# Another order of work inside a batch body: keys at steps 4 and 7, values together at step 5, sums of two steps joined

## The chip, the cores and the metric

One core of one Trainium2 chip. The time is device microseconds (us) of one execution; lower is better. The core has TensorE (PE, matrix products; its weight loads are shown as PEld), VectorE (DVE), ScalarE (ACT), GpSimd (POOL) and SyncE (SP, which here only issues DMAs). Each works through its own instruction list in order and waits on semaphores that the others raise.

## The reference

A block of three parts for 16 batches of 64 query tokens of width 128. Only the first part, a cross attention, is touched by the change:

```python
x = x + xattn(layernorm(x), ctx, ctx)        # ctx: (16 batches, 1601 keys, 128)
q, k, v = (t.reshape(b, -1, 16, 8).transpose(0, 2, 1, 3) for t in (x@Wq.T+bq, ctx@Wk.T+bk, ctx@Wv.T+bv))
weights = softmax(q @ k.T / sqrt(8))         # 16 heads of 8
out = (weights @ v) @ Wo.T + bo
x = x + mamba_mlp(layernorm(x), ...)         # state space model, then an MLP
x = x + experts(layernorm(x), ...)           # 8 gated experts, two chosen per token
```

## The kernel before, in words

`attention` runs 16 **bodies**, one for a batch (index `i`), each of 13 **steps** (`k`), one for every 128 keys (the last has 65). The order of everything is written out by hand and the same list of steps is walked by each engine. In one step TensorE does some of these:

- `scores(i, k)` (L647): 8 bf16 matmuls, transposed scores of 128 keys against 16 heads x 64 queries, into two of three halves `score`. ScalarE then does two exps (L836), one for each half (p = 0, 1), into `probs` (4 slots). `scores` of a step may start once the first exp of the step before is done.
- `sum_values(b, s)` (L667): weights times values of step s, with a column of ones for the denominators; fp32, into the bank `sums`. It needs both exps of s. At the end of a batch ScalarE copies `sums` out (`sums_out`, L826).
- `maxima(b, u)` (L596): unit u of 16 of a *later* batch: a rough pass of scores, 2 x 401 columns into one of the two buffers of `wide`, of which VectorE takes the row maximum (L911). After u = 15 come `row_maxima` (L920), `turn_max` (L604, a transpose) and `shifts` (L928, L930); SyncE sends the shift to `q_cur` (L352), and `scores` of the next batch needs it.
- `keys(i + 3, half)` (L515 to L517 with 401 columns): projection of the keys of a later batch, two halves, into `wide`; ScalarE copies each out (`keys_out`, L818) to `k_full`, GpSimd splits that into bf16 high and low parts (`split_keys`, L438, L441), SyncE lays them into `k_stack` (L320).
- `vals(i + 2, half)` (L515 to L517 with 128 columns): projection of the values, 7 and 6 blocks of 128 keys, into `wide`; VectorE copies each half out (`vals_out`, L907). GpSimd's `split(i + 4)` (L425, L428) waits for the second half.

`wide` is a **ring of two buffers**: the users come in the order of `ring_order()`, and each waits until the one two places before it has been emptied, by VectorE (units, values, turned maxima) or by ScalarE (keys).

A body in steady state before the change, as the loop at L695 and `units_at` with `LEAD = 5` give it (m = unit, s = sums of that step, s11 and s12 are of the batch before):

```
step  0: m7 s11      1: m8 s12     2: m9 values0     3: m10 s0 s1 m11    4: m12 s2
step  5: m13 s3 values1            6: m14 s4 keys0   7: m15 s5           8: m0 s6 keys1 m1
step  9: m2 s7 turn 10: m3 s8     11: m4 s9         12: m5 s10 m6
```

Bodies 1 to 12 have all of it. Body 0 has its own table (two units in each of steps 0 to 7, keys at 9 and 11, turn at 10, no values), body 13 has no keys, body 14 neither keys nor values, body 15 no units; bodies 14 and 15 also turn finished sums and project tokens (`tail_at`). ScalarE does `keys_out` and `sums_out` after both exps of their step.

Of the kernel before, what the change touches and what calls it, by code (L numbers as in the profile page):

```python
# [12 lines left out]
B, LQ, LK = 16, 64, 1601  # L13
# [11 lines left out]
NK = (LK + P - 1) // P  # L25
# [3 lines left out]
VW, VH = GH * HD + 2, GH - 1  # L29
NPROB, NSCORE, NSLOT, NQ = 4, 3, 3, 4  # L30
PREFETCH = 3
LEAD = 5
M_LOW, M_SIGN, M_FIRST = 2, 3, 4
V_STEPS, K_STEPS = (2, 5), (6, 8)
P_STEPS, C_STEPS = (3, 6), (8, 9, 11, 12)
TAIL = 10
NSPARE = 4
# [15 lines left out]
def keys_of(k):  # L53
    return min(P, LK - k * P)


def units_at(i, k):

    found = []
    for b in (i + 1, i + 2):  # L60
        lead = {1: 0, 2: 3}.get(b, LEAD)
        found += [(b, u) for u in range(16) if 1 <= b < B and
                  NK * (b - 1) - lead + (lead + 8) * u // 16 == NK * i + k]
    return found


def keys_at(i, k):

    steps = K_STEPS if i else (9, 11)
    return [(i + PREFETCH, steps.index(k))] if k in steps and i + PREFETCH < B else []  # L70


def turn_step(i):

    return 9 if i else 10


def tail_at(i, k):


    at = NK * (i - B + 2) + k - TAIL
    found = [("w", p, 0) for p in range(3) if at == 5 * p + 5]
    found += [("s", p, at - 5 * p) for p in range(3) if at in (5 * p, 5 * p + 1)]
    return found + [("o", p, 0) for p in range(3) if at == 5 * p + 4]
# [15 lines left out]
def ring_order():  # L100

    order = [("k", 0, 0), ("k", 0, 1), ("x", 0, 0), ("q", 0, 0)]
    order += [("m", 0, u) for u in range(16)] + [("t", 0, 0), ("v", 2, 0), ("v", 2, 1)]
    for i in range(B):
        for k in range(NK):
            order += [("m",) + unit for unit in units_at(i, k)[:1]]
            if k in V_STEPS and 0 < i < B - 2:
                order += [("v", i + 2, V_STEPS.index(k))]
            order += [("k",) + half for half in keys_at(i, k)]
            order += [("m",) + unit for unit in units_at(i, k)[1:]]  # L110
            if k == turn_step(i) and i + 1 < B:
                order += [("t", i + 1, 0)]
            order += [what for what in tail_at(i, k) if what[0] != "w" and what[2] == 0]
    return order
# [27 lines left out]
def attention(nc, A, keep):  # L142


    with ExitStack() as ctx:
# [366 lines left out]
        def _(pe):  # L512
# [52 lines left out]
            def keys(b, half):  # L565
                n, w = b % 2, half_free(pe, ("k", b, half))
                if b == 0:
                    pe.wait_ge(s_low0, half + 1)
                elif half == 0:
                    pe.wait_ge(s_split, b)  # L570
                for c in range(2):
                    at = CH * (2 * half + c)
                    last = product3(wide[:, w, 512 * c:512 * c + CH], wkv_hi[:, 0, :], wkv_lo[:, 0, :],
                                    ctx_hi[:, n, at:at + CH], ctx_lo[:, n, at:at + CH])
                last.then_inc(s_wide, 1)

            def vals(b, half):
                n, w = b % 2, half_free(pe, ("v", b, half))
                for k in range(7 * half, 7 + 6 * half):
                    at = P * (k - 7 * half)  # L580
                    ks = slice(k * P, k * P + P)
                    last = product3(wide[:, w, at:at + P], ctx_hi[:, n, ks], ctx_lo[:, n, ks],
                                    wkv_hi[:, 1, :], wkv_lo[:, 1, :])
                last.then_inc(s_wide, 1)
# [69 lines left out]
            def sum_values(b, k):  # L654
                n, m, slot = b % NSLOT, keys_of(k), (NK * b + k) % NPROB
                if k == 0:
                    if b < 2:
                        spare_emptied(pe, ("v", b, 3))
                    else:
                        is_empty(pe, ("v", b, 1))  # L660
                    if b:
                        pe.wait_ge(s_sums, b)
                pe.wait_ge(s_exp, 2 * (NK * b + k) + 2)
                for c, (first, heads) in enumerate(((0, VH), (VH, 1))):
                    for g in range(G):
                        q = (GH * g + first) * LQ
                        last = pe.matmul(sums[32 * g:32 * g + 32, first * LQ:(first + heads) * LQ],  # L667
                                         values[0:m, n, k, VW * g + 2 * c:VW * g + 2 * c + 32],
                                         probs[0:m, slot, q:q + heads * LQ],
                                         start=(k == 0 and c == 0), stop=(k == NK - 1), skip_group_check=True)  # L670
                last.then_inc(s_pv, 1)
# [23 lines left out]
            for i in range(B):  # L695
                for k in range(NK):
                    scores(i, k)
                    units = units_at(i, k)
                    if units:
                        maxima(*units[0])  # L700
                    if i >= 1 and k < 2:
                        sum_values(i - 1, NK - 2 + k)
                    if k == 3:
                        sum_values(i, 0)
                    if k >= 3:
                        sum_values(i, k - 2)
                    if k in V_STEPS and 0 < i < B - 2:
                        vals(i + 2, V_STEPS.index(k))
                    for half in keys_at(i, k):
                        keys(*half)  # L710
                    for unit in units[1:]:
                        maxima(*unit)
                    if k == turn_step(i) and i + 1 < B:
                        turn_max(i + 1)
                    for kind, p, t in tail_at(i, k):
                        if kind == "s":
                            turn_sums(p, t)
                        elif kind == "o":
                            turn_tokens(p)
                        else:  # L720
                            project_tokens(p)
# [6 lines left out]
        def _(act):  # L728
# [93 lines left out]
            def sums_out(b):  # L822
                act.wait_ge(s_pv, NK * (b + 1))
                if b == 0:
                    act.wait_ge(s_qlow, len(LATE_Q))
                nc.scalar.copy(keep.sums[:, :, b * LQ:b * LQ + LQ],  # L826
                               sums[:, 0:GH * LQ].rearrange("p (j q) -> p j q", j=GH)).then_inc(s_sums, 1)

            for i in range(B):
                for k in range(NK):  # L830
                    m, step = keys_of(k), NK * i + k
                    for p in range(2):
                        act.wait_ge(s_score, 2 * step + p + 1)
                        if p == 0 and step >= NPROB:
                            act.wait_ge(s_pv, step - NPROB + 1)
                        nc.scalar.activation(  # L836
                            probs[0:m, step % NPROB, :].rearrange("r (g p c) -> r p g c", g=G, p=2)[:, p],
                            score[0:m, (2 * step + p) % NSCORE, :].rearrange("r (g c) -> r g c", g=G), ACT.Exp,
                            scale=HD ** -0.5).then_inc(s_exp, 1)
                    if i >= 1 and k == 1:  # L840
                        sums_out(i - 1)
                    for half in keys_at(i, k):
                        keys_out(*half)
            sums_out(B - 1)
            nc.scalar.activation(root_of_one[:], one[:], ACT.Sqrt)

# [1 line left out]
        def _(dve):  # L848
# [164 lines left out]
            for i in range(B):  # L1013
                for k in range(NK):
                    units = units_at(i, k)
                    for b, u in units[:1]:
                        maximum(b, u)
                        if u == 15:
                            row_maxima(b)
                    if k in V_STEPS and 0 < i < B - 2:  # L1020
                        vals_out(i + 2, V_STEPS.index(k))
                    for b, u in units[1:]:
                        maximum(b, u)
                        if u == 15:
                            row_maxima(b)
                    if k == turn_step(i) and i + 1 < B:
                        shifts(i + 1)
                    for kind, p, t in tail_at(i, k):
                        if kind == "s":
                            if t == 1:  # L1030
                                divide(p)
                        elif kind == "o":
                            tokens_out(p)
                        else:
                            residual(p)
# [1142 lines left out]
```

## Time and profile before

| | |
|---|---|
| median of 3 runs (lowest to highest) | 572.72 us (571.77 to 573.69) |
| the profiled execution: its time | 574.46 us |
| its span, first to last instruction | 572.6 us |
| busy: PE, PEld, DVE, ACT, POOL | 91%, 59%, 73%, 66%, 57% |

The span is shorter than the execution's time by what lies around the instructions. Attention takes the first 386 us or so; the two later parts are not touched. Busy shares are averages over all stages; a busy PE is not a PE at its peak, since matmuls overlap. In the timeline a row is: start, length, engine, line, operation, how many were merged, and in brackets how long the engine was idle before it and whose work ended that.

### The profile page before, as it was taken

To read this page: it belongs to the slowest core of one execution; us is meant where nothing else is said; L and a number is where in the kernel's file an instruction comes from. 1 tells how busy PE (TensorE), PEld (TensorE's weight loads), DVE (VectorE), ACT (ScalarE), POOL (GpSimd) and SP (SyncE) were. 2 spreads that over 40 slices of the span, in tenths; PEclk is the share of its full clock that TensorE was granted. 3 is DMA by queue.
4 is the path that set the end of the run, shared out by engine and by line. 5 is a ranking of instruction groups with operands and counts; after the bars stand their busy time and mean duration, and the time that the engine had idled before them with its cause. 6 is when DMAs were issued, how large, how long until landed. Compare 5 with 4: busy or idle time off the path is not lost. (4 is left out here: it accounts for less than half of the span.)

```text
span 572.6 us, 18926 instructions
## 1 busy us (share of the span) xinstructions
PE 520.9 (91%) x7882; PEld 338.6 (59%) x7882; DVE 419.7 (73%) x749; ACT 380.4 (66%) x704; POOL 323.6 (57%) x197
## 2 busy tenths in 40 slices
PE   3887999999999999999999999999999869999997
PEld 1534565565565565565565565665375736777776
DVE  6287888797797798788788799447877567455554
ACT  4883668678678678778778778873844426656662
POOL 1698878558558558558657299204000035667673
PEclk9897999999999999999999999999989979999999
DMA  6776444354354354354352463002000000000001
GB/s 210 137 154 132 124 112 96 91 119 93 87 121 96 81 120 97 83 119 98 81 119 49 107 145 84 3 2 101 2 1 2 1 1 1 2 2 0 0 0 38
DMA packets 17962, 41.64 MB, mean 73 GB/s; under 512 B 5542, under 2 KB 8366, under 8 KB 17770
## 3 DMA queue, kind: packets, MB, share of 16 engines
q1 hardware_dynamic: 17144, 40.10, 30.2%
q8 instruction: 59, 0.97, 0.8%
q10 hardware_dynamic: 740, 0.42, 0.2%
q14 instruction: 19, 0.16, 0.1%
HBM read 19.70 MB, written 0.52 MB: 35 GB/s over the span
## 5 line engine op out<-in xcount | busy, mean ns | idle before, releaser
L911 DVE TENSOR_REDUCE half_max<-wide 128x2 f32<-128x802 f32 x256 | 241.6, 988 | 42.8 <-PE wide L596 38.8
L836 ACT ACTIVATE probs<-score 128x512 f32<-128x512 f32 (+1 forms) x416 | 225.8, 596 | 66.6 <-PE score L647 66.3
L667 PE MATMUL sums<-probs,values 128*32 128x192 f32 (+3 forms) x3328 | 131.6, 280 | 0.0
L667 PEld LDWEIGHTS sums<-probs,values 128*32 128x32 f32 (+1 forms) x3328 | 86.9, 110 | 51.4 <-issue 22.6
L596 PE MATMUL wide<-k_stack,q_cur 48*128 48x401 bf16 x512 | 87.5, 339 | 12.6 <-ACT k_full L818 6.2
L647 PE MATMUL score<-q_cur,k_stack 50*128 50x128 bf16 (+1 forms) x1664 | 82.7, 219 | 7.3 <-ACT probs L836 6.3
L425 POOL TENSOR_TENSOR ctx_hi<-ctx_in,one 128x1601 bf16<-128x1601 f32 x15 | 42.9, 2857 | 76.9 <-PE wide L517 67.8
L1904 POOL TENSOR_TENSOR hid_lo<-hid_e,hid_hi 114x512 bf16<-114x512 f32 x47 | 54.1, 1156 | 35.5 <-ACT hid_hi L1928 34.3
L647 PEld LDWEIGHTS score<-q_cur,k_stack 50*128 50x128 bf16 (+1 forms) x1664 | 51.9, 95 | 32.7 <-ACT probs L836 12.9
L2039 DVE SCALAR_TENSOR_TENSOR hid_e<-gu,keep_bgu,gate 114x512 f32<-114x512 f32 x48 | 35.9, 750 | 40.1 <-ACT gate L1941 40.0
L438 POOL TENSOR_TENSOR k_hi<-k_full,one 128x1601 bf16<-128x1601 f32 x15 | 42.8, 2856 | 31.0 <-ACT k_full L818 24.9
L1941 ACT ACTIVATE gate<-gu,gate_bias 114x512 f32<-114x512 f32 x48 | 32.9, 687 | 37.0 <-PE gu L1874 34.7
L428 POOL TENSOR_TENSOR ctx_lo<-ctx_in,ctx_hi 128x1601 bf16<-128x1601 f32 x15 | 48.6, 3242 | 1.2
L441 POOL TENSOR_TENSOR k_lo<-k_full,k_hi 128x1601 bf16<-128x1601 f32 x15 | 48.6, 3239 | 1.2
L596 PEld LDWEIGHTS wide<-k_stack,q_cur 48*128 48x128 bf16 x512 | 24.8, 93 | 38.1 <-DVE half_max L911 16.7
L1872 PE MATMUL gu<-keep_t_hi,keep_w_hi 128*114 128x512 bf16 x96 | 37.6, 392 | 4.9 <-DVE hid_e L2039 4.9
L907 DVE COPY values<-wide 128x896 f32<-128x896 f32 (+1 forms) x28 | 28.7, 1024 | 15.4 <-PE wide L517 15.3
L818 ACT ACTIVATE k_full<-wide,keep_vecs 128x802 f32<-128x802 f32 x26 | 24.2, 929 | 22.1 <-PE wide L517 22.1
L1873 PE MATMUL gu<-keep_t_lo,keep_w_hi 128*114 128x512 bf16 x96 | 37.3, 389 | 0.0
L1874 PE MATMUL gu<-keep_t_hi,keep_w_lo 128*114 128x512 bf16 x96 | 37.2, 388 | 0.0
L515 PE MATMUL wide<-wkv_hi,ctx_hi 128*128 128x128 bf16 x182 | 33.4, 225 | 2.9 <-DVE half_max L911 2.9
L1889 POOL MEMSET one<- 114x1 f32 x1 | 0.1, 99 | 63.5 <-POOLq L1043 63.5
(327 smaller groups left out, 919.1 us busy)
## 6 DMA issues: line engine op xcount, KB each, us to landing
k_stack<-k_hi SPq DMA_DIRECT2D x128, 102.0 KB, 3.4
ctx_in<-in_ctx SPq DMA_DIRECT2D x56, 200.1 KB, 3.4
k_stack<-k_lo SPq DMA_DIRECT2D x64, 102.0 KB, 3.2
ctx_in<-in_wgu SPq DMA_DIRECT2D x16, 171.0 KB, 3.4
keep_w<-in_w SPq DMA_DIRECT2D x1, 1368.0 KB
ctx_in<-in_ctx SPq DMA_DIRECT2D x1, 800.5 KB, 8.4
keep_x<-in_x SPq DMA_DIRECT2D x1, 512.0 KB, 7.0
q_cur<-shift SPq DMA_DIRECT2D x30, 2.0 KB
```

What stands on the lines that cost most here:

```text
L425: pool.tensor_tensor(ctx_hi[:, n, 0:LK], ctx_in[:, n, :], one[:].to_broadcast([P, LK]), ALU.mult).then_inc(s_splithi, 1)
L428: pool.tensor_tensor(ctx_lo[:, n, 0:LK], ctx_in[:, n, :], ctx_hi[:, n, 0:LK], ALU.subtract).then_inc(s_split, 1)
L438: pool.tensor_tensor(k_hi[:, 0:LK], k_full[:, 0:LK], one[:].to_broadcast([P, LK]), ALU.mult).then_inc(s_khi, 1)
L441: pool.tensor_tensor(k_lo[:, 0:LK], k_full[:, 0:LK], k_hi[:, 0:LK], ALU.subtract).then_inc(s_klo, 1)
L596: last = pe.matmul(wide[:, w, 512 * p:512 * p + CH], q_cur[half:half + TERM, b % NQ, g].rearrange("p h q -> p (h q)"), k_stack[half:half + ...
L647: last = pe.matmul(score[0:m, (2 * step + p) % NSCORE, P * g:P * g + P], k_stack[half:half + TERM + 2, n, g, k * P:k * P + m], q_cur[half: ...
L667: last = pe.matmul(sums[32 * g:32 * g + 32, first * LQ:(first + heads) * LQ], values[0:m, n, k, VW * g + 2 * c:VW * g + 2 * c + 32], probs ...
L836: nc.scalar.activation(probs[0:m, step % NPROB, :].rearrange("r (g p c) -> r p g c", g=G, p=2)[:, p], score[0:m, (2 * step + p) % NSCORE, ...
L911: dve.tensor_reduce(half_max[:, b % 2, :, u // 4, u % 4], wide[:, w, :].rearrange("p (c k) -> p c k", c=2)[:, :, 0:CH], AX.X, ALU.max).the ...
L1872: pe.matmul(o, hi, t_hi[:, half], start=True, stop=False)
L1873: pe.matmul(o, hi, t_lo[:, half], start=False, stop=False)
L1904: pool.tensor_tensor(hid_lo[:, par, h, n, :], hid[:, n, :], hid_hi[:, par, h, n, :], ALU.subtract).then_inc(s["lo"], 1)
```

## The change

The steps get a new table; no operation is added or taken away. In steady state:

```
step  0: m6 s11 m7   1: s12 m8     2: m9 s0 s1 m10   3: s2 m11           4: keys0 m12 s3
step  5: m13 values0 values1       6: m14 s4 s5      7: m15 keys1        8: m0 s6 turn
step  9: m1 s7 m2   10: s8 m3     11: m4 s9         12: m5 s10
```

The units of batches 1 and 2 keep their places. On ScalarE `keys0` is now copied out between the two exps of its step, `keys1` after them, and `sums_out` between the two exps of step 1.

```diff
-LEAD = 5
-V_STEPS, K_STEPS = (2, 5), (6, 8)
+V_STEP, K_STEPS = 5, (4, 7)
+UNIT_STEPS = (8, 9, 9, 10, 11, 12, 13, 13, 14, 15, 15, 16, 17, 18, 19, 20)
+SUM_STEPS = (2, 2, 3, 4, 6, 6, 8, 9, 10, 11, 12, 13, 14)
+SUMS_BEFORE_MAXIMA = (1, 3, 10)
...
-        lead = {1: 0, 2: 3}.get(b, LEAD)
-        found += [(b, u) for u in range(16) if 1 <= b < B and
-                  NK * (b - 1) - lead + (lead + 8) * u // 16 == NK * i + k]
+        lead = {1: 0, 2: 3}.get(b)
+        found += [(b, u) for u in range(16) if 1 <= b < B and NK * i + k == (
+            NK * (b - 2) + UNIT_STEPS[u] if lead is None else NK * (b - 1) - lead + (lead + 8) * u // 16)]
+def sums_at(i, k):
+    return [(b, s) for b in (i - 1, i) if b >= 0 for s in range(NK) if NK * (b - i) + SUM_STEPS[s] == k]
 def turn_step(i):
-    return 9 if i else 10
+    return 8 if i else 10
...
                     scores(i, k)
                     units = units_at(i, k)
+                    for b, half in keys_at(i, k):
+                        if half == 0:
+                            keys(b, half)
+                    if k in SUMS_BEFORE_MAXIMA:
+                        for b, s in sums_at(i, k):
+                            sum_values(b, s)
                     if units:
                         maxima(*units[0])
-                    if i >= 1 and k < 2:
-                        sum_values(i - 1, NK - 2 + k)
-                    if k == 3:
-                        sum_values(i, 0)
-                    if k >= 3:
-                        sum_values(i, k - 2)
-                    if k in V_STEPS and 0 < i < B - 2:
-                        vals(i + 2, V_STEPS.index(k))
-                    for half in keys_at(i, k):
-                        keys(*half)
+                    if k == V_STEP and 0 < i < B - 2:
+                        for half in range(2):
+                            vals(i + 2, half)
+                    for b, half in keys_at(i, k):
+                        if half == 1:
+                            keys(b, half)
+                    if k not in SUMS_BEFORE_MAXIMA:
+                        for b, s in sums_at(i, k):
+                            sum_values(b, s)
                     for unit in units[1:]:
                         maxima(*unit)
...
                             scale=HD ** -0.5).then_inc(s_exp, 1)
-                    if i >= 1 and k == 1:
-                        sums_out(i - 1)
-                    for half in keys_at(i, k):
-                        keys_out(*half)
+                        if i >= 1 and k == 1 and p == 0:
+                            sums_out(i - 1)
+                        for b, half in keys_at(i, k):
+                            if half == p:
+                                keys_out(b, half)
```

`ring_order()` and VectorE's loop follow the same table.

## Rows read from the trace of the kernel before

**Rows 1.** Timeline of DVE, the `shifts` of bodies 1, 12 and 13
```profile
92.76 0.27 DVE L928 CAST shift_hi<-wide 16x128 bf16<-16x128 f32 x1
...
327.56 0.27 DVE L928 CAST shift_hi<-wide 16x128 bf16<-16x128 f32 x1
346.27 0.27 DVE L928 CAST shift_hi<-wide 16x128 bf16<-16x128 f32 x1
```
**Rows 2.** Busy time by stretch: one whole body
```profile
221.14:242.48 21.34, 20.10 (x399) 12.87 (x397) 17.82 (x23) 15.90 (x30) 13.98 (x7) 1.00 0.45 100
```
**Rows 3.** Timeline of PE in that stage: two plain steps
```profile
200.48 0.40 PE L647 MATMUL score<-q_cur,k_stack 50*128 50x128 bf16 x8
200.72 0.34 PE L596 MATMUL wide<-k_stack,q_cur 48*128 48x401 bf16 x2
200.98 0.65 PE L667 MATMUL sums<-probs,values 128*32 128x192 f32 x16
201.56 0.41 PE L647 MATMUL score<-q_cur,k_stack 50*65 50x128 bf16 x8
```
**Rows 4.** Timeline of PE: values (step 2), joined sums and an extra unit (step 3)
```profile
205.94 0.10 PEld L515 LDWEIGHTS wide<-wkv_hi,ctx_hi 128*128 128x128 bf16 x1 [0.48 <-DVE half_max L911]
...
207.22 0.40 PE L647 MATMUL score<-q_cur,k_stack 50*128 50x128 bf16 x8
...
207.72 1.08 PE L667 MATMUL sums<-probs,values 128*32 128x192 f32 x32
208.73 0.34 PE L596 MATMUL wide<-k_stack,q_cur 48*128 48x401 bf16 x2
208.91 0.39 PE L647 MATMUL score<-q_cur,k_stack 50*128 50x128 bf16 x8
```
**Rows 5.** Timeline of PE: keys (step 6), then the turn (step 9)
```profile
213.53 0.34 PE L515 MATMUL wide<-ctx_hi,wkv_hi 128*128 128x401 bf16 x1
...
214.66 0.40 PE L647 MATMUL score<-q_cur,k_stack 50*128 50x128 bf16 x8
...
220.27 0.38 PE L604 MATMUL wide<-nident,row_max 128*16 128x128 f32 x2
220.59 0.40 PE L647 MATMUL score<-q_cur,k_stack 50*128 50x128 bf16 x8
```
**Rows 6.** Timeline of PE in body 0, scores followed at once by sums
```profile
64.01 0.39 PE L647 MATMUL score<-q_cur,k_stack 50*128 50x128 bf16 x8
64.33 0.64 PE L667 MATMUL sums<-probs,values 128*32 128x192 f32 x16
```
**Rows 7.** Waits, 199.24 to 220.58 us (one body): us in total, times, longest
```profile
PEld score L647 <- ACT probs L836: 0.8, 2, 0.6
PEld wide L596 <- ACT k_full L818: 0.7, 1, 0.7
PEld wide L596 <- DVE half_max L911: 0.6, 3, 0.2
```
**Rows 8.** Timeline of ACT: `sums_out`, `keys_out`
```profile
205.49 0.38 ACT L826 COPY keep_sums<-sums 128x256 f32<-128x256 f32 x1
...
218.55 0.93 ACT L818 ACTIVATE k_full<-wide,keep_vecs 128x802 f32<-128x802 f32 x1 [0.80 <-PE wide L517]
219.38 1.08 ACT L836 ACTIVATE probs<-score 128x512 f32<-128x512 f32 x2
```
**Rows 9.** Timeline of DVE: units back to back, a copy of values
```profile
200.28 6.50 DVE L911 TENSOR_REDUCE half_max<-wide 128x2 f32<-128x802 f32 x7
207.32 1.09 DVE L907 COPY values<-wide 128x896 f32<-128x896 f32 x1 [0.54 <-PE wide L517]
```
**Rows 10.** Timeline of POOL: first of `split`, last of `split_keys`
```profile
212.63 2.86 POOL L425 TENSOR_TENSOR ctx_hi<-ctx_in,one 128x1601 bf16<-128x1601 f32 x1 [6.45 <-PE wide L517]
...
222.49 3.25 POOL L441 TENSOR_TENSOR k_lo<-k_full,k_hi 128x1601 bf16<-128x1601 f32 x1
```
**Rows 11.** Busy time by stretch, in body 0 (columns as in rows 2)
```profile
54.90:58.00 3.10, 3.10 (x48) 1.86 (x46) 2.20 (x3) 0.83 (x3) 3.02 (x2) 0.53 0.88 143
```

More of the change, by code:

```diff
@@ L105, in ring_order @@
         for k in range(NK):
+            order += [("k",) + half for half in keys_at(i, k) if half[1] == 0]
             order += [("m",) + unit for unit in units_at(i, k)[:1]]
-            if k in V_STEPS and 0 < i < B - 2:
-                order += [("v", i + 2, V_STEPS.index(k))]
-            order += [("k",) + half for half in keys_at(i, k)]
+            if k == V_STEP and 0 < i < B - 2:
+                order += [("v", i + 2, half) for half in range(2)]
+            order += [("k",) + half for half in keys_at(i, k) if half[1] == 1]
             order += [("m",) + unit for unit in units_at(i, k)[1:]]
@@ L698, in _ @@
                     units = units_at(i, k)
+                    for b, half in keys_at(i, k):
[4 more added lines that the diff above has]
+                            sum_values(b, s)
                     if units:
                         maxima(*units[0])
-                    if i >= 1 and k < 2:
-                        sum_values(i - 1, NK - 2 + k)
-                    if k == 3:
-                        sum_values(i, 0)
-                    if k >= 3:
-                        sum_values(i, k - 2)
-                    if k in V_STEPS and 0 < i < B - 2:
-                        vals(i + 2, V_STEPS.index(k))
-                    for half in keys_at(i, k):
-                        keys(*half)
+                    if k == V_STEP and 0 < i < B - 2:
+                        for half in range(2):
[6 more added lines that the diff above has]
+                            sum_values(b, s)
                     for unit in units[1:]:
@@ L1019, in _ @@
                             row_maxima(b)
-                    if k in V_STEPS and 0 < i < B - 2:
-                        vals_out(i + 2, V_STEPS.index(k))
+                    if k == V_STEP and 0 < i < B - 2:
+                        for half in range(2):
+                            vals_out(i + 2, half)
                     for b, u in units[1:]:
```

## The prediction
> **What bounds the kernel now.** I read the page for the place of the change, then the timeline of VectorE for the period of a body, the busy time of one body, TensorE's timeline through one body, and last the waits of that body.
>
> The shifts of bodies 1 and 12 lie 327.56 - 92.76 = 234.80 us apart, eleven bodies: 21.345 us for a body; the next, without keys, takes 18.71 [rows 1]. In one body the engines are busy 20.10 (PE), 12.87 (PEld), 17.82 (DVE), 15.90 (ACT), 13.98 (POOL), and the granted clock is 1.00, which is 2.4 GHz [rows 2]. Nothing is full by busy time, so I count what TensorE must issue, from start to start of its instructions:
>
> - scores to unit 0.24, unit to sums 0.26, sums to next scores 0.58: a plain step is 1.08 [rows 3]. The two exps of a step take 1.08 on ACT as well [rows 8], so ACT has no slack in a plain step and much in a long one.
> - Values, 7 blocks: 205.94 to 207.22, 1.28; by blocks the second half is 6/7 of it, 1.10. Joined sums 1.01 instead of 2 x 0.58 = 1.16, saving 0.15. An extra unit at the end of a step 0.18 [rows 4].
> - Half the keys 1.13, the turn 0.32 [rows 5]. Scores followed at once by sums 0.32 [rows 6], so a step with the sums first is 0.32 + 0.58 + 0.18 = 1.08 too.
>
> A body before has 13 plain steps' worth (14.04), 3 extra units (0.54), two halves of keys (2.26), values (2.38), the turn (0.32), less one joined sum (0.15): 19.39. The period is 21.345, so TensorE stands still for **1.95 us a body**. The waits say where: for exps 0.8 (scores after a key copy), for `k_full` 0.7 (the unit behind keys1 in step 9), for VectorE 0.6 in three units [rows 7], and 0.48 ahead of values0 [rows 4]. That makes 2.6, more than 1.95 because a late weight load is partly covered by matmuls still running. TensorE is the bound at 91%, and every wait is for a buffer that an evacuating engine still holds.
>
> A rule speaks against this reading. The Trainium skill, Perfetto Trace Analysis, section Identifying the Most-Contended Engine, says that TensorE's matmul busy share is no good measure and that the load share is to be used; by it TensorE (12.87 of 21.34, 60%) would be far from full and VectorE (83%) the engine to relieve. It would leave up to 3.5 us a body to gain, not 1.95. The trace agrees that busy time overstates PE, but small moving tiles keep it from issuing faster than the starts above.
>
> **The change, part by part.** No instruction is added. What TensorE must issue in a body: 19.39 less another 0.15 for the second joined pair = 19.24. By step, 0 to 12: 1.26, 1.08, 1.69, 1.08, 2.21, 2.88, 1.51, 1.63, 1.40, 1.26, 1.08, 1.08, 1.08. For the waits I walk once through the ring and the exps. Rates: a reader starts 0.10 after TensorE's next start (207.22 to 207.32) and units on DVE are 0.92 apart, 0.99 long; the sixth of the seven ends at 205.87 and values start at 205.94, so a buffer comes back 0.07 after its reader ends [rows 4, 9]. Values copies 1.09 and about 1.0 [rows 9]. A key copy is 0.93, an exp can start 0.83 after it [rows 8]. Zero is the scores of step 5.
>
> - **Step 5**, m13 0.24, values0 0.50, values1 1.78, end 2.88. m13's reduce ends at 1.60, before values1. The copies end at 2.97 and 3.95. ACT has its two exps only and then idles some 1.5 us: no cost, as its 15.90 busy leave 4 us a body. Before, each half of values cost a wait or an ACT gap of its own.
> - **Step 6**, m14 at 3.12 finds the copied buffer back at 3.04; its reduce waits behind the second copy, 3.95 to 4.94. Joined sums keep TensorE busy meanwhile; step 7 starts at 4.39.
> - **Step 7**, m15 4.63, keys1 wants m14's buffer at 4.89 and gets it at 5.01: **wait 0.12**. Step 8 starts 6.14.
> - **Step 8**, keys1 is copied 6.25 to 7.18. The turn needs that buffer (7.25) and TensorE comes to it at 7.22. The exp queued behind the copy runs 7.08 to 7.62, and scores 9 need it: 7.69 against 7.54, **wait 0.15**. What was 0.5 ahead of step 8's scores and 0.5 behind keys1 is now covered by sums 6 and the turn.
> - **Steps 9 to 12**, DVE: m0, the two shifts (together about 0.75), m1 from 8.55, m2 ends 10.46. m4 wants its buffer at 10.27 and gets 10.53: **wait 0.26**. Step 0 starts 12.45.
> - **Steps 0 to 4**, `sums_out` (0.38 [rows 8]) sits between the exps of step 1, from about 1.05 after its scores, and ends before sums 0 start at 1.6; with the old place on ACT it would end near 2.0 and be late. m7's reduce ends at 15.06, m9 wants that buffer at 15.03: **wait 0.10**. Exps of step 2 end about 0.2 before sums 2 want them. keys0 in step 4 goes ahead of m12, whose buffer waits for nothing. Its copy delays only the second exp, and sums 4 come two steps later. Step 5 starts at 19.87.
>
> Waits 0.63 a body, period 19.87. Four places pass with under 0.1 to spare (m13 behind the key copy, m14, keys0, the turn); bounds for them are 0 and 0.1 each, and I take 0.10 in all. Period 19.97, **gain 1.38 us a body, 16.6 us in the 12 full bodies**.
>
> The rest: body 13 keeps the values and loses no key; step 7 then has neither sums nor keys and is held at 1.08 by the exps instead of 0.50, so it gains less, 0.6 (bounds 0 and 1.2). Bodies 14 and 15 are held by the exps; two joined pairs instead of one are longer on TensorE than on ACT by up to 0.4, and the steps without sums give nothing back: +0.5 together (0 to 1). Body 0 is held by VectorE with two units a step, 0. There the clock stands at 0.53 for 3.1 us (1.2 GHz for nearly all of it), after a stretch in which TensorE had only scores and units [rows 11]; sums one step earlier could shift or shorten it: -1.5 to +1, taken as 0. Sum: -16.6 - 0.6 + 0.5 = **-16.7 us**.
>
> Other queues: SyncE's steps are tied to the scores, so they contract with the body. The turn one step earlier puts the shift's DMAs some 3.5 us ahead of the scores that need it. GpSimd's `split` still starts when values end; in the timeline `k_lo` ends 225.74 - 212.63 = 13.1 us after it starts [rows 10], and with the keys earlier it no longer waits for them.
>
> Span 572.6 - 16.7 = 555.9, time of that execution 574.46 - 16.7 = 557.8; against the median, which is 1.7 lower, **556.0 us**.
>
> **Rivals.**
>
> - *VectorE becomes the bound.* My walk leaves it about 2 us idle a body, and two of four waits are already for it, with the 11 units from step 9 to step 3 at 0.92 filling 10.1 us in which TensorE issues 10.0. If each handover is slower, or the shifts or the second copy of values push the queue back by another 0.2 or so in three or four places, a body takes 20.6: gain 0.7 x 12 and the rest as above, 564. For: its 17.82 busy. Against: it idles before units and copies now. The skill's rule above would favour it, and by that rule the trace is not yet decided. Chance 0.2.
> - *All near misses pass.* Waits 0.4 a body and the slow clock in body 0 gone: 12 x 1.7 + 1.5 = 22, so 551. Chance 0.1.
> - *Slower, through k_full.* `keys_out` of half 0 may overwrite `k_full` only when GpSimd has written `k_lo` of the batch before, and it now sits between two exps: if it waits, the second exp, then the scores of step 6, wait with it. `split` starts at about 3.1, so `k_lo` ends near 3.1 + 13.1 - 0.7 = 15.5; the copy comes at 17.66 + 0.24 + 1.24 = 19.1. The room falls to 3.6 us; before, it was 213.53 + 21.34 + 1.24 - 225.74 = 10.4. Above 3.6 every further us of lateness is a us a body; from 5.0 the kernel is slower; at 6, 12 x 1 = 12 us more, 585. For: the keys moved two steps earlier, the values ended later. Against: GpSimd's operations have kept one duration all along. With whatever else turns the sign: chance 0.07.
> - *Nothing moves*: TensorE is full by its starts and the waits only change place, period near 21.3, 573. It would need 1.3 us of waits that the walk doesn't show. Chance 0.03.
>
> **How the numbers follow.** Forecast 0.6, VectorE bound 0.2, near misses pass 0.1, slower 0.07, nothing 0.03. The likeliest case by itself is 552 to 560; the range goes to the middle of the VectorE case and the edge of the better one, 551 to 564. Faster by over 0.3% (1.7 us, about what can be told from no change): 0.9; within it 0.03; slower 0.07.
>
> **What would show it.** Shifts 20.0 us apart (20.6: VectorE). PE busy per body unchanged near 20. The wait of a unit for `k_full` (0.7) and of the values for `half_max` (0.5) gone; small waits of units for `half_max` in steps 11 and 2; an ACT gap of some 1.5 us in each step 6. GpSimd's wait ahead of `k_hi` (before: for `k_full`) gone. A wait of `k_full` for GpSimd's `k_lo` would prove the slower case; a period above 20.3 would make the walk wrong, and its step is the one whose wait stands longest in the list.

## The result and the profile after

| | before | changed |
|---|---|---|
| median (lowest to highest) | 573.21 us (571.77 to 574.86), 4 runs | 556.0 us (552.94 to 559.36), 4 runs |
| ratio to before | | 0.9706, 95% interval 0.9677 to 0.9736 |
| the profiled execution: time, span | 574.46, 572.6 | 557.50, 555.7 |
| busy: PE, PEld, DVE, ACT, POOL | 91%, 59%, 73%, 66%, 57% | 92%, 61%, 76%, 69%, 58% |

The kernel is 3% faster, and its median is the predicted 556.0 us. Ratios here and below are of fast runs alone (of all runs one, 576.95 us in the first experiment, was slow). Each experiment had the kernel before run beside it (medians 571.53, 572.56 and 573.26 us for the three groups), so experiments are compared by ratio and by period, and their times only roughly.

The period of a body in the timeline of VectorE, as in [rows 1]:

```profile
92.86 0.27 DVE L946 CAST shift_hi<-wide 16x128 bf16<-16x128 f32 x1
...
310.13 0.27 DVE L946 CAST shift_hi<-wide 16x128 bf16<-16x128 f32 x1
328.72 0.27 DVE L946 CAST shift_hi<-wide 16x128 bf16<-16x128 f32 x1
```

Eleven bodies take 310.13 - 92.86 = 217.27 us, 19.75 each, against 21.345: **1.60 us less a body**. Busy time of one body (columns as in [rows 2]: the stretch, its length, then the busy time of PE, PEld, DVE, ACT and POOL with the count of instructions, and last the granted clock, the share of time the DMA engines work and GB/s):

```profile
191.61:211.36 19.75, 19.62 (x397) 12.98 (x397) 17.90 (x23) 16.01 (x31) 13.93 (x7) 1.00 0.44 108
```

VectorE, ScalarE and GpSimd are busy for what they were before, within 0.11 us, in a body 1.6 us shorter, at the same clock. PE shows 19.62 instead of 20.10; the prediction had it unchanged. The waits of that body, to be set beside [rows 7]:

```profile
PEld sums L679 <- ACT probs L853: 0.8, 4, 0.2
...
PEld score L659 <- ACT probs L853: 0.7, 2, 0.4
PEld wide L527 <- DVE half_max L929: 0.5, 2, 0.3
...
PEld wide L608 <- DVE half_max L929: 0.3, 1, 0.3
```

The unit's wait for `k_full` is gone, the 0.48 ahead of values is 0.25, the longest wait of scores for an exp fell from 0.6 to 0.4 (in total only from 0.8 to 0.7). Step 5 and what follows, PE:

```profile
203.80 0.40 PE L659 MATMUL score<-q_cur,k_stack 50*128 50x128 bf16 x8
204.04 0.35 PE L608 MATMUL wide<-k_stack,q_cur 48*128 48x401 bf16 x2
204.39 0.23 PE L527 MATMUL wide<-wkv_hi,ctx_hi 128*128 128x128 bf16 x1
...
206.67 0.40 PE L659 MATMUL score<-q_cur,k_stack 50*128 50x128 bf16 x8
206.92 0.34 PE L608 MATMUL wide<-k_stack,q_cur 48*128 48x401 bf16 x2
207.19 1.08 PE L679 MATMUL sums<-probs,values 128*32 128x192 f32 x32
208.21 0.40 PE L659 MATMUL score<-q_cur,k_stack 50*128 50x128 bf16 x8
...
209.84 0.40 PE L659 MATMUL score<-q_cur,k_stack 50*128 50x128 bf16 x8
210.07 0.34 PE L608 MATMUL wide<-k_stack,q_cur 48*128 48x401 bf16 x2
210.34 0.65 PE L679 MATMUL sums<-probs,values 128*32 128x192 f32 x16
210.93 0.39 PE L616 MATMUL wide<-nident,row_max 128*16 128x128 f32 x2
211.42 0.40 PE L659 MATMUL score<-q_cur,k_stack 50*128 50x128 bf16 x8
```

Both halves of the values run through in 2.28 us without a gap; the keys of step 7 too. One stop is ahead of the last row, 0.49 after the turn instead of 0.32: the scores wait for the exp behind the key copy. Another is ahead of the turn itself, which starts 0.59 after its sums, where before the change it started 0.46 after them (219.81 to 220.27): the copy of keys1 ends at 209.95 + 0.93 = 210.88, and the turn, which needs that buffer, starts at 210.93. The same on ACT and DVE:

```profile
207.10 1.09 ACT L853 ACTIVATE probs<-score 128x512 f32<-128x512 f32 x2 [1.66 <-PE score L659]
208.64 1.08 ACT L853 ACTIVATE probs<-score 128x512 f32<-128x512 f32 x2 [0.45 <-PE score L659]
209.95 0.93 ACT L835 ACTIVATE k_full<-wide,keep_vecs 128x802 f32<-128x802 f32 x1 [0.22 <-PE wide L529]
210.77 2.16 ACT L853 ACTIVATE probs<-score 128x512 f32<-128x512 f32 x4
```

```profile
205.77 1.96 DVE L925 COPY values<-wide 128x896 f32<-128x896 f32 x2 [0.35 <-PE wide L529]
207.65 0.98 DVE L929 TENSOR_REDUCE half_max<-wide 128x2 f32<-128x802 f32 x1
...
212.16 10.29 DVE L929 TENSOR_REDUCE half_max<-wide 128x2 f32<-128x802 f32 x11
```

The ACT gap behind the values is 1.66 us, and VectorE works eleven units on end, those issued from step 9 to step 3.

**Where 16.9 us of span went.** I cut both profiles at the scores of step 12 (65 rows high, `50x65`), the last of each body. Examples, of before and then of the changed kernel:

```profile
71.67 0.41 PE L647 MATMUL score<-q_cur,k_stack 50*65 50x128 bf16 x8
...
94.83 0.41 PE L647 MATMUL score<-q_cur,k_stack 50*65 50x128 bf16 x8
```

```profile
73.93 0.41 PE L659 MATMUL score<-q_cur,k_stack 50*65 50x128 bf16 x8
...
96.45 0.41 PE L659 MATMUL score<-q_cur,k_stack 50*65 50x128 bf16 x8
```

| stretch | before | changed | difference |
|---|---|---|---|
| to the first scores | 49.35 | 49.79 | +0.44 |
| body 0 | 22.32 | 24.14 | +1.82 |
| body 1 | 23.16 | 22.52 | -0.64 |
| bodies 2 to 12 | 234.80 | 217.27 | -17.53 |
| body 13 | 18.71 | 18.58 | -0.13 |
| bodies 14, 15 | 33.53 | 34.37 | +0.84 |
| all behind the attention | 190.7 | 189.0 | -1.7 |

The code of the first row and the last is untouched, so these differences are not the change's. The low clock of body 0 lay elsewhere in the two profiles (before at 54.9 to 58, [rows 11]) and lasted longer in the second; after:

```profile
50.00:54.00 4.00, 3.47 (x34) 1.32 (x29) 3.30 (x4) 2.54 (x5) 4.00 (x3) 0.50 0.42 95
54.00:58.00 4.00, 4.00 (x72) 2.54 (x70) 2.59 (x4) 1.80 (x4) 3.92 (x3) 0.66 0.65 144
```

### The profile page after: what moved, and what is told of

It is laid out like the page before. It is cut to its first block and busy times, and to the rows that moved or that the text cites. A ratio compares the mean times of both kernels' runs of the same rounds, so it can differ in the third digit from the quotient of the medians.

```text
span 555.7 us, 18926 instructions
## 1 busy us (share of the span) xinstructions
PE 512.7 (92%) x7882; PEld 338.8 (61%) x7882; DVE 419.9 (76%) x749; ACT 382.0 (69%) x704; POOL 323.0 (58%) x197
## 5 line engine op out<-in xcount | busy, mean ns | idle before, releaser
L679 PE MATMUL sums<-probs,values 128*32 128x192 f32 (+3 forms) x3328 | 128.0, 279 | 0.0
L527 PE MATMUL wide<-wkv_hi,ctx_hi 128*128 128x128 bf16 x182 | 31.4, 220 | 0.5 <-DVE half_max L929 0.5
L1851 PE MATMUL down<-w_hi,hid_hi 114*128 (+1 forms) x180 | 31.7, 219 | 0.0
```

## The experiments

The numbers measured are the period of a steady body, from shift to shift, and the time. The first six each undo one part of the change and leave the rest; the first also contains the edit of the sixth, the order of sums and unit inside a step.

**Sums by the old table.**

```diff
-SUM_STEPS = (2, 2, 3, 4, 6, 6, 8, 9, 10, 11, 12, 13, 14)
-SUMS_BEFORE_MAXIMA = (1, 3, 10)
+SUM_STEPS = (3, 3, 4, 5, 6, 7, 8, 9, 10, 11, 12, 13, 14)
+SUMS_BEFORE_MAXIMA = ()
```

> The changed kernel, but the sums as before: sums 0 and 1 joined at step 3, the sums of step k-2 at step k, always behind the first unit. In the changed kernel a steady body takes 19.75 us (shift to shift). My theory, that TensorE's own issue time plus its waits make the body: one joined pair less costs 0.15, and sums now stand behind 2.4 us of values (step 5) or keys (step 7), so the exps late after a key copy are no longer covered: 20.1 to 20.6, whole time 4 to 10 us above 556. Rival, the joining brings only the 0.15 us of TensorE that it saves: 19.90, 2 us above.

Measured: 21.25 a body (195.21 to 216.47), 573.66 us, ratio to before 1.003 (1.0003 to 1.0057). Nearly the whole gain is gone, 1.50 of 1.60 us a body, more than either theory said; the time is above both as well. (The profiled execution, 567.40 us, was the fastest of ten.) Its PE timeline shows what I had left out: step 2 now holds scores and two units, 0.65 us of work, and takes 1.55, held by VectorE and the exps; the sums it might have done make steps 3, 5 and 7 longer.

```profile
202.68 0.40 PE L659 MATMUL score<-q_cur,k_stack 50*128 50x128 bf16 x8
202.91 0.34 PE L608 MATMUL wide<-k_stack,q_cur 48*128 48x401 bf16 x2
203.63 0.34 PE L608 MATMUL wide<-k_stack,q_cur 48*128 48x401 bf16 x2 [0.38 <-DVE half_max L929]
204.23 0.40 PE L659 MATMUL score<-q_cur,k_stack 50*128 50x128 bf16 x8 [0.26 <-ACT probs L853]
```

Step lengths against the changed kernel: step 2 -0.15, 3 +0.52, 5 +0.57, 6 -0.45, 7 +0.65, 8 -0.30, 9 to 1 +0.6 together. Sums moved out of a step that is then short give nothing back; in the step they move to they cost 0.52 to 0.65. About 0.5 of the 1.5 is the order of sums and unit, which the sixth experiment takes alone.

**Keys at steps 6 and 8.**

```diff
-V_STEP, K_STEPS = 5, (4, 7)
+V_STEP, K_STEPS = 5, (6, 8)
```

> The changed kernel, but keys at steps 6 and 8 again. My theory: the turn (step 8) must now wait for the copy of the keys issued in the same step, and the joined sums of step 6 delay the keys; waits on key copies come back, body 20.4 to 20.9, 564 to 570 us. Rival, the place of the keys is indifferent because ScalarE has 3.7 us of slack in a body: 19.8, 556 to 557.

Measured: 20.75, 570.52 us (just above my range), 0.9984 (0.9957 to 1.0012). The period is in my range and half of the cause is as I had it: waits behind key copies come back. But the turn does not wait (it starts 0.47 after its sums), and values wait for VectorE, which I had not foreseen, because the keys no longer stand ahead of them in step 4. The longest waits of TensorE in that body are 0.80 of scores for an exp and 0.74 of values for a unit's buffer:

```profile
207.56 0.10 PEld L527 LDWEIGHTS wide<-wkv_hi,ctx_hi 128*128 128x128 bf16 x1 [0.74 <-DVE half_max L929]
...
213.67 0.23 PEld L659 LDWEIGHTS score<-q_cur,k_stack 50*128 50x128 bf16 x8 [0.80 <-ACT probs L853]
```

**Values at steps 2 and 5.**

```diff
-            if k == V_STEP and 0 < i < B - 2:
-                order += [("v", i + 2, half) for half in range(2)]
+            if k in V_STEPS and 0 < i < B - 2:
+                order += [("v", i + 2, V_STEPS.index(k))]
```

(and the same in TensorE's and VectorE's loops, with `V_STEPS = (2, 5)`)

> The changed kernel, but the halves of the values at steps 2 and 5 again. My theory: step 2 lies inside VectorE's unbroken run of units, so the values must wait there for a buffer (0.4 to 0.6 as before the change) and steps 5 to 7 lose nothing: body 20.1 to 20.5, 560 to 565 us. Rival, that VectorE is the bound and its order of copies and maxima is indifferent: 19.75 +- 0.1, 556.

Measured: 20.60 and 568.42 us, both above my ranges, 0.9943 (0.9921 to 0.9965). The wait of the values is where I put it, in VectorE's run of units, but 0.94 instead of 0.4 to 0.6:

```profile
203.50 0.10 PEld L527 LDWEIGHTS wide<-wkv_hi,ctx_hi 128*128 128x128 bf16 x1 [0.94 <-DVE half_max L928]
```

**Units and turn at their old steps.**

```diff
-UNIT_STEPS = (8, 9, 9, 10, 11, 12, 13, 13, 14, 15, 15, 16, 17, 18, 19, 20)
+UNIT_STEPS = (8, 8, 9, 10, 11, 12, 12, 13, 14, 15, 16, 16, 17, 18, 19, 20)
...
-    return 8 if i else 10
+    return 9 if i else 10
```

> The changed kernel, but the units of batches from 3 on at their old steps (u1 with u0 at step 8, u6 at 12, u10 and u11 at 3) and the turn at step 9. My theory: each moved unit brings a wait of 0.1 to 0.2 for VectorE where two units meet a short step: body 19.95 to 20.3, 558 to 562 us. Rival, the units' table does not matter as VectorE has to do 16 of them in any case: 19.75.

Measured: 20.86, 571.69 us, 1.0004 (0.9982 to 1.0025): 1.11 of 1.60 us a body gone, where I expected 0.2 to 0.55, and by the time the whole gain; bodies 13 and 14 are each 1.0 to 1.1 us longer too. Units 10 and 11 both stand in step 3, right ahead of keys0 of step 4, which needs unit 10's buffer: TensorE stands still for most of a reduce, and step 4 is 3.07 us long instead of 2.31, which is 0.76 of the 1.11.

```profile
207.46 0.10 PEld L527 LDWEIGHTS wide<-ctx_hi,wkv_hi 128*128 128x128 bf16 x1 [0.87 <-DVE half_max L929]
```

**ScalarE's copies after both exps.**

```diff
-                        if i >= 1 and k == 1 and p == 0:
-                            sums_out(i - 1)
-                        for b, half in keys_at(i, k):
-                            if half == p:
-                                keys_out(b, half)
+                    if i >= 1 and k == 1:
+                        sums_out(i - 1)
+                    for b, half in keys_at(i, k):
+                        keys_out(b, half)
```

> The changed kernel, but ScalarE copies keys and sums out after both exps of their step, as before. My theory: the copy of the sums then ends about 2.0 after the scores of step 1 and the joined sums 0 of step 2 want their bank at 1.6, a wait of 0.3 to 0.4; the copy of keys0 starts 0.3 later and m13 waits as long: body 20.2 to 20.5, 561 to 565 us. Rival, ScalarE's order inside a step is hidden by the other half of the scores: 19.75 to 19.85, 556 to 557.

Measured: 20.05, 561.75 us, 0.9812 (0.9768 to 0.9856). The period is between both theories. The joined sums do wait for the copy of `sums`: they start 0.56 after the unit ahead of them instead of 0.27, and step 2 is 1.99 us long instead of 1.69, the whole 0.30. But m13 doesn't wait: both exps of step 4 end at 205.89, and keys0 is copied from 205.93, 0.10 behind m12's start as in the changed kernel, so the copy starts no later.

**The unit always first.**

```diff
-SUMS_BEFORE_MAXIMA = (1, 3, 10)
+SUMS_BEFORE_MAXIMA = ()
```

> The changed kernel, but the sums never ahead of the first unit (steps 1, 3 and 10 as the others). Steady body: sums 12 come 0.26 later, so the copy of the sums too, and units 8 and 11 ask for their buffer 0.6 earlier, when VectorE still has it: 19.9 to 20.2. In body 0 step 10 the unit is no longer held up behind the sums and the turn behind it comes sooner: 0.3 to 0.7 us less there. Whole: 557 to 560 us. Rival, the order of sums and units inside a step is indifferent: 19.75 in the body, and body 0 as it is.

Measured: 20.235, 559.78 us, 0.977 (0.9721 to 0.9819). The body as in my theory, a little above its range: steps 1, 2 and 10 are 0.18, 0.12 and 0.30 longer, step 11 is 0.13 shorter. In body 0 step 10 goes from 2.67 us to 1.98 (65.93 to 67.91 us), the 0.7 expected.

**Batches 0, 14 and 15 with the old table of sums.**

```diff
+EDGE_STEPS = (3, 3, 4, 5, 6, 7, 8, 9, 10, 11, 12, 13, 14)
...
-    return [(b, s) for b in (i - 1, i) if b >= 0 for s in range(NK) if NK * (b - i) + SUM_STEPS[s] == k]
+    return [(b, s) for b in (i - 1, i) if b >= 0 for s in range(NK)
+            if NK * (b - i) + (SUM_STEPS if 0 < b < B - 2 else EDGE_STEPS)[s] == k]
...
+def sums_first(i, k):
+    return k in SUMS_BEFORE_MAXIMA and (0 < i < B - 2 or i == B - 2 and k == 1)
...
-                    if k in SUMS_BEFORE_MAXIMA:
+                    if sums_first(i, k):
...
-                    if k not in SUMS_BEFORE_MAXIMA:
+                    if not sums_first(i, k):
```

> The changed kernel, but batches 0, 14 and 15 have the old table of sums (joined at step 3 only) and the sums go behind the unit in their bodies. The changed kernel's body 0 is 1.4 us, bodies 14 and 15 together 0.9 us longer than before the change in the two profiles. My theory: this is the table (joined sums that TensorE can't hide, steps 5 and 7 held by the exps), so bodies 14 and 15 lose 0.9 and body 0 at least 0.6: 1.5 to 2.3 us off, about 554. Rival, body 0's loss is where the slow clock fell, which changes from run to run: then only 0.9 off.

Measured: 19.75, 554.96 us, 0.9711 (0.9678 to 0.9743). Body 0, from its first scores to those of step 12, is 22.75 instead of 24.14; step 10 is 1.99 us in place of 2.67. Bodies 14 and 15 hardly gain: 16.66 and 17.46 against 16.46 and 17.91, 0.25 together where I expected 0.9. My theory is right for step 10 of body 0 and wrong for the last two bodies. The other 0.71 of body 0 lies in steps 0 to 7, where the clock is low for a while, and is not shown to be the table's: the profiles of the changed kernel and of the second to fourth experiments, whose code for body 0 is the same, take 23.95 to 24.85 us for it. By its time the kernel can't be told from the changed one, the intervals being nearly the same.

**Less work for TensorE.**

```diff
-                    last = product3(wide[:, w, 512 * c:512 * c + CH], wkv_hi[:, 0, :], wkv_lo[:, 0, :],
-                                    ctx_hi[:, n, at:at + CH], ctx_lo[:, n, at:at + CH])
+                    o = wide[:, w, 512 * c:512 * c + CH]
+                    pe.matmul(o, wkv_hi[:, 0, :], ctx_hi[:, n, at:at + CH], start=True, stop=False)
+                    last = pe.matmul(o, wkv_hi[:, 0, :], ctx_lo[:, n, at:at + CH], start=False, stop=True)
```

> The changed kernel with the third product of the keys (high part of the context times low part of the weights) left out in the 12 to 13 bodies that project keys in the ring: four matmuls of 401 columns, 0.17 us apart, 0.69 us of TensorE a body; its keys are less precise. If TensorE is the bound: 19.1 to 19.3 a body, 548 to 550 us. If VectorE is the bound: 19.65 to 19.75, 555 us or more.

Measured: 19.35 (188.62 to 207.97), 550.95 us, 0.9643 (0.9602 to 0.9684). 0.40 of 0.69 us comes through, a little less than the theory of a TensorE bound had. By steps: step 7 is 0.34 shorter, step 4 only 0.20, and step 11 grows by 0.13, its unit waiting for VectorE. So TensorE is the bound in most of the places where this work lies, not in all.

**Less work for VectorE.**

```diff
-                                  wide[:, w, :].rearrange("p (c k) -> p c k", c=2)[:, :, 0:CH],
+                                  wide[:, w, :].rearrange("p (c k) -> p c k", c=2)[:, :, 0:CH - 40],
```

> The changed kernel with each of VectorE's maxima taken over 2 x 361 instead of 2 x 401 columns (the last 40 of each half are left out, so the shift may be smaller than the true maximum): 16 reduces of 0.99 become about 0.91, some 1.3 us of VectorE less a body. If TensorE bounds the body and VectorE counts only in the 0.5 us of waits that TensorE has for it: 19.3 to 19.6 a body, 550 to 554 us. If VectorE is the bound (its 17.9 us and its turn-arounds): 18.4 to 18.8. Taking 0.69 us off TensorE gave 0.40.

Measured: 19.56, 550.13 us, 0.9626 (0.9575 to 0.9676). VectorE's busy time falls by 1.03 us (expected: 1.3) and the body by 0.19:

```profile
187.35:206.91 19.56, 19.44 (x397) 12.90 (x397) 16.87 (x23) 16.01 (x31) 13.93 (x7) 1.00 0.45 110
```

A microsecond off TensorE is worth 0.58 (0.40 / 0.69), one off VectorE 0.18 (0.19 / 1.03). No run takes work off ScalarE. In the plain steps its two exps take 1.08 us, as long as TensorE's starts, and in the body shown it works from 210.77 to 218.42 us, through steps 9 to 12, 0 and 1, with two gaps of 0.16 and 0.18 us. So these steps may be bound by ScalarE as much as by TensorE; which one is not shown. The time is lower than eleven bodies at 0.19 make it. In its profile the scores of step 12 of body 0 come 3.0 us earlier than in the changed kernel's (70.96 against 73.93): 1.9 of this lies ahead of the first scores, which come at 47.93 instead of 49.79, and 1.1 in body 0, where VectorE has two units a step and the low clock falls differently, which I can't tell apart. Bodies 1, 13 and 14 are 1.1 us shorter together.

**The new table of sums alone, in the kernel before.**

```diff
+SUM_STEPS = (2, 2, 3, 4, 6, 6, 8, 9, 10, 11, 12, 13, 14)
...
-                    if i >= 1 and k < 2:
-                        sum_values(i - 1, NK - 2 + k)
-                    if k == 3:
-                        sum_values(i, 0)
-                    if k >= 3:
-                        sum_values(i, k - 2)
+                    for b in (i - 1, i):
+                        for s in range(NK):
+                            if b >= 0 and NK * (b - i) + SUM_STEPS[s] == k:
+                                sum_values(b, s)
```

> The kernel before the change with the new table of sums alone (joined at steps 2 and 6; none at 5 and 7). All other work stands where it was. Undoing one part of the change each time took back 0.3 to 1.5 us of a body, 5.2 in all, while the whole brings 1.6; so the parts should be worth little alone. Here step 7 has only a unit and is held by the exps at 1.08 instead of 0.5, and sums 0 and 1 stand behind the values of step 2: 21.3 to 22.0 a body (before 21.345), 571 to 580 us. Rival, parts that each pay: 1.5 less at once, 19.9.

Measured: 22.65 (208.79 to 231.44), 590.82 us, 1.0294 (1.0244 to 1.0343): one part of the change alone makes the kernel 3% slower, more than my range said. Against the kernel before, the steps that gained sums grow: step 2, with values and the joined sums, by 1.05 (to 3.09 us), and step 6 by 0.40; step 4, with as much as before, by 0.26. The steps that have less now give back 0.25 (step 3), 0.13 (step 5) and 0.01 (step 7). Step 7:

```profile
225.28 0.40 PE L648 MATMUL score<-q_cur,k_stack 50*128 50x128 bf16 x8
225.51 0.34 PE L597 MATMUL wide<-k_stack,q_cur 48*128 48x401 bf16 x2
226.85 0.40 PE L648 MATMUL score<-q_cur,k_stack 50*128 50x128 bf16 x8 [1.01 <-ACT probs L835]
```

TensorE has only scores and a unit there, while ScalarE copies the keys of step 6 and only then does the exp that the next scores need; taking 0.58 us of sums out of the step turned them into waiting.

**Units of batch 2 on the new table too.** On top of the seventh:

```diff
+UNIT_STEPS_2 = (10, 10, 11, 11, 12, 12, 13, 13, 14, 15, 15, 16, 17, 18, 19, 20)
...
-        lead = {1: 0, 2: 3}.get(b)
-        found += [(b, u) for u in range(16) if 1 <= b < B and NK * i + k == (
-            NK * (b - 2) + UNIT_STEPS[u] if lead is None else NK * (b - 1) - lead + (lead + 8) * u // 16)]
+        found += [(b, u) for u in range(16) if 1 <= b < B and NK * i + k == (
+            u // 2 if b == 1 else NK * (b - 2) + (UNIT_STEPS if b > 2 else UNIT_STEPS_2)[u])]
```

> The kernel of e7 (batches 0, 14 and 15 with the old table of sums), and the units of batch 2 brought onto the new table from step 0 of body 1 on: u0 to u5 in pairs at steps 10, 11 and 12 of body 0, one more than before in body 0. Body 1 takes 22.5 us in the changed kernel against 19.75 of the next ones. If that is the shifted units of batch 2: body 1 20.0 to 20.8, body 0 longer by about 0.9 (one unit more for VectorE), 552.5 to 554 us. Rival, body 1 is long for what body 0 leaves late (stacks, keys): it stays at 22 or more, 555 to 556.

Measured: 553.78 us, 0.9656 (0.962 to 0.9693). Body 1 20.86 instead of 22.52, at the edge of my range; body 0 22.94 against 22.75 in the seventh, so the extra unit cost 0.2 rather than 0.9.

**And the first of them one step earlier.**

```diff
-UNIT_STEPS_2 = (10, 10, 11, 11, 12, 12, 13, 13, 14, 15, 15, 16, 17, 18, 19, 20)
+UNIT_STEPS_2 = (9, 10, 10, 11, 12, 12, 13, 13, 14, 15, 15, 16, 17, 18, 19, 20)
```

> As e11, but the first unit of batch 2 at step 9 of body 0 already, u1 and u2 at 10, u3 at 11, u4 and u5 at 12. VectorE stands idle in steps 8 and 9 of body 0, so the extra unit costs nothing there: 0.5 to 1 us better than e11. Rival, the unit shares the ring with keys0 of step 9 and delays them and the exps behind: equal to e11 or up to 1 us worse.

Measured: 552.87 us, 0.9665 (0.9623 to 0.9708). Bodies 0 and 1 together take 91.61 - 48.19 = 43.42 us against 46.66 in the changed kernel:

```profile
71.22 0.41 PE L666 MATMUL score<-q_cur,k_stack 50*65 50x128 bf16 x8
91.61 0.41 PE L666 MATMUL score<-q_cur,k_stack 50*65 50x128 bf16 x8
```

Against the eleventh it is 0.4 us the better over these two bodies, less than profiles of the same code for body 0 differ by, so neither theory is told from the other. It has the lowest median of the versions with full work, 3 us under the changed kernel, but by ratio the eleventh is as good (0.9656), and both intervals overlap the changed kernel's (0.9677 to 0.9736), so that they beat it is likely and not shown.

## Why the prediction was right, step by step

**The bound.** That TensorE's starts fill most of the body holds: its rate of 0.58 a microsecond against VectorE's 0.18, and a period of 19.75 and not 20.6, tell the forecast from the first rival. It is not shown for the plain steps, where ScalarE is as full. The rule of the Trainium skill (Perfetto Trace Analysis, Identifying the Most-Contended Engine) would, by the share of weight loads, have had me relieve VectorE, at 83% before and 91% (17.90 of 19.75) after, ahead of TensorE at 60% and 66%. The trace doesn't agree: taking 1.03 us off VectorE gave 0.19, taking 0.69 us of matmuls off TensorE gave 0.40. For this kernel of small matmuls the count of starts was the better measure.

**The walk.** Each step's length, predicted with its waits and then as measured from scores to scores:

| step | 5 | 6 | 7 | 8 | 9 | 10 | 11 | 12 | 0 | 1 | 2 | 3 | 4 | sum |
|---|---|---|---|---|---|---|---|---|---|---|---|---|---|---|
| predicted | 2.88 | 1.51 | 1.75 | 1.55 | 1.26 | 1.08 | 1.34 | 1.08 | 1.26 | 1.08 | 1.79 | 1.08 | 2.21 | 19.87 |
| measured | 2.87 | 1.54 | 1.63 | 1.58 | 1.25 | 1.08 | 1.21 | 1.18 | 1.26 | 1.07 | 1.70 | 1.07 | 2.31 | 19.75 |

The wait ahead of scores 9 is there (0.15 predicted, 0.17). keys1 hardly waits, since two copies of values take 1.96 together and not 2.1; m9 doesn't either. m4's wait is 0.13, half of what I had. Steps 4 and 12 are 0.10 longer than planned: in step 4, keys that follow directly on scores start 0.33 behind them and not 0.24; for step 12 I have no reason. The 0.10 that I added for near misses was not needed: 1.60 a body, not 1.38.

One price of the walk was wrong. I took the turn at 0.32, its own start to the next scores. But it starts 0.46 after its sums (219.81 to 220.27), where scores would start 0.58 after them, so it adds only 0.20, and TensorE's starts come to 19.27 a body before and 19.12 in the plan, 0.12 less each. The sum of step 8 came out right all the same because the turn then waited 0.13 for the key copy, a wait that I had at nothing. That is luck.

**Twelve full bodies** was wrong, and so was **body 0 at nothing**. Only 11 are alike: body 1 still has batch 2's units on the old table (the change keeps it), and gave 0.64, not 1.38. There units 9 and 10 stand in step 3 ahead of keys0, which then waits 0.87 us for VectorE, as in the fourth experiment; the eleventh, with those units moved, makes body 1 1.66 us shorter. In body 0 the sums ahead of the unit in step 10 hold up the turn (0.7, the sixth and seventh experiments). Its step 11 is 0.33 longer, in the seventh experiment too: the keys there now come ahead of the sums and wait 0.27 for VectorE, which no run isolates. The remaining 0.8 of its 1.82 lies in steps 0 to 9 with the low clock and stays open. Bodies 14 and 15 cost 0.84 where I had 0.5. Body 13 gave 0.13 instead of 0.6. Its step 7 is 1.08 as I had it; what I missed is step 5, 3.31 us long instead of 2.87. With no keys in step 4, the values come to VectorE's run of units too early, the same wait as in the second experiment:

```profile
322.16 0.10 PEld L527 LDWEIGHTS wide<-wkv_hi,ctx_hi 128*128 128x128 bf16 x1 [0.74 <-DVE half_max L929]
```

In sum these terms were 3.8 us too good (0.7 in body 1, 1.8 in body 0, 0.5 in body 13, 0.3 in the last two, 0.4 ahead of the first scores), the eleven steady bodies at 0.22 each 2.4 too poor, and 1.7 came from untouched code: that the forecast of 16.7 comes so close to the 16.9 of the profiles is luck, errors that cancel. The mechanism and the main term are not.

**k_full.** The room came out as worked out. In the body shown `split` starts at 206.89 and `k_lo` ends at 219.20, and the next key copy is due 203.05 + 19.75 = 222.80: 3.60 us, predicted 3.6. GpSimd no longer waits ahead of `k_hi`:

```profile
206.89 2.86 POOL L437 TENSOR_TENSOR ctx_hi<-ctx_in,one 128x1601 bf16<-128x1601 f32 x1 [5.67 <-PE wide L529]
209.83 3.24 POOL L440 TENSOR_TENSOR ctx_lo<-ctx_in,ctx_hi 128x1601 bf16<-128x1601 f32 x1
213.02 2.85 POOL L450 TENSOR_TENSOR k_hi<-k_full,one 128x1601 bf16<-128x1601 f32 x1
215.96 3.24 POOL L453 TENSOR_TENSOR k_lo<-k_full,k_hi 128x1601 bf16<-128x1601 f32 x1
```

What the prediction did not see, and its experiments missed by, is how far the parts depend on each other. Undone singly they take 1.50, 1.00, 0.85, 1.11, 0.30 and 0.49 us a body back. The last is contained in the first; without it the sum is 4.8 where the whole brings 1.6, and the table of sums alone loses 1.3.

## What to carry to other kernels

Where engines run in lockstep by a written order, walk through one period with the start-to-start times of the trace, buffer by buffer; it gave the period to 0.12 us of 19.75 (0.22 with the allowance for near misses), in part because errors in single steps cancelled. Judge an order only as a whole: a step must hold at least what the slowest partner does in it, because work taken out of an already short step gives little or nothing back, and two users of a two-buffer ring directly ahead of a third cost most of a read-out. Count the irregular bodies at both ends by themselves, step by step: taking work out of one (the keys of body 13) can expose a wait that it had covered.

## What the runs showed of the hardware

A stretch of low clock (1.2 GHz, granted 0.50) in body 0 came in the profile of every kernel here, but not at one place and not of one length: 0.53 over 54.9 to 58 us before the change; 0.50 over 50 to 54 and 0.66 over 54 to 58 after it, where TensorE had been busy for 1.15 of 4.00 us over 46 to 50. In the eleventh experiment one more lay in body 14, which took 18.15 us against 16.66 in the seventh, with the same sums and units. Just ahead of it, over 331 to 333, TensorE was busy for 1.27 of 2.00 us:

```profile
331.00:333.00 2.00, 1.27 (x25) 0.74 (x22) 1.96 (x3) 1.93 (x6) 1.92 (x2) 1.00 0.00 0
333.00:339.00 6.00, 5.71 (x104) 3.43 (x108) 4.17 (x6) 3.57 (x7) 5.92 (x3) 0.72 0.02 4
```

The same code took different times in the profiles: the stretch to the first scores 47.8 to 49.8 us (the scores wait there, 0.2 to 2.9 us, for the DMA that brings the shift to `q_cur`), everything behind the last scores of step 12 186.1 to 191.3 us. What sets these was not tried and stays open; they are as large as the small terms above.
